# Layer 1's QKV projection: the bias through PE, the rotation of q and k on DVE alone

## The reference

```python
h = _layernorm(x) * (1 + ca) + sa
qkv = h @ w_qkv.T + b_qkv                      # 512 -> 768: 32 q heads, 8 k heads, 8 v heads of 16
q, k, v = split(qkv, [512, 640])
def apply_rope(x):                             # per head, pairs (even, odd)
    xr, xi = x[..., 0::2], x[..., 1::2]
    return stack([xr * cos - xi * sin, xr * sin + xi * cos])   # cos, sin of position * inv_freq, 8 values
q, k = apply_rope(q), apply_rope(k)
```

## Time and profile before

| | us |
|---|---|
| median of 3 runs (1818.61 to 1824.83) | 1823.09 |
| the profiled execution | 1821.3 |
| its span, first to last instruction | 1819.0 |
| PE busy | 1673.6 (92%) |
| DVE busy | 1203.1 (66%) |
| ACT busy | 1009.0 (55%) |
| POOL busy | 734.8 (40%) |

### The profile page before, as it was taken

The page is one execution under the profiler, slowest core; times in us unless marked ns, Lnnn a source line. Parts: engine busy times, 40 slices in busy tenths (PEclk is TensorE's granted clock), DMA queues, the critical chain, the costliest instruction groups (busy, mean ns, idle before and its releaser), DMA issues. The chain is left out here.

```text
span 1819.0 us, 28423 instructions
## 1 busy us (share of the span) xinstructions
PE 1673.6 (92%) x10091; PEld 1339.6 (74%) x10091; DVE 1203.1 (66%) x2930; ACT 1009.0 (55%) x2229; POOL 734.8 (40%) x660
## 2 busy tenths in 40 slices
PE   5599999999999999999997699997769999999778
PEld 3488999999999999899885588785645555554557
DVE  6867777777776777777667533345886777763475
ACT  3377777777777778777772311102216666666131
POOL 1486575766757567475531200000542222211200
PEclk9899999999999999999998799998959999999889
DMA  5000000100000100100002211005000000000021
GB/s 177 29 13 29 19 24 19 30 30 19 25 25 24 30 19 25 30 13 24 19 7 80 74 53 53 14 0 183 1 1 1 1 1 1 1 1 1 30 45 47
DMA packets 70772, 55.27 MB, mean 30 GB/s; under 512 B 22974, under 2 KB 52862, under 8 KB 70634
## 3 DMA queue, kind: packets, MB, share of 16 engines
q1 hardware_dynamic: 70634, 53.47, 10.0%
HBM read 51.36 MB, written 2.10 MB: 29 GB/s over the span
## 5 line engine op out<-in xcount | busy, mean ns | idle before, releaser
L698 PEld LDWEIGHTS psum<-a_probsT,a_v 128*128 128x128 f32 x2304 | 295.3, 192 | 25.5 <-issue 3.8
L698 PE MATMUL psum<-a_probsT,a_v 128*128 128x128 f32 x2304 | 299.9, 275 | 1.7 <-ACT a_probsT L896 1.5
L793 DVE CUSTOM_DVE_ANT_0 psum<-psum,a_keys_allowed 128x128 f32<-128x128 f32 (+7 forms) x256 | 195.7, 765 | 80.8 <-PE psum L77 72.0
L879 ACT ACTIVATE a_probs<-psum,a_neg_max 128x128 f32<-128x128 f32 (+7 forms) x256 | 190.8, 745 | 64.8 <-DVE a_neg_max L793 56.6
L1763 ACT ACTIVATE a_probsT<-psum 128x512 f32<-128x512 f32 (+3 forms) x384 | 174.2, 497 | 86.9 <-PE psum L1600 62.8
L888 ACT ACTIVATE a_probs<-a_probs,a_row_inv 128x128 f32<-128x128 f32 (+7 forms) x256 | 201.3, 786 | 21.9 <-DVE a_row_inv L800 21.4
L568 POOL TENSOR_TENSOR a_turned_pool<-a_q_sum,a_sine 64x512 f32<-64x512 f32 x62 | 79.3, 1279 | 273.3 <-DVE a_q_sum L779 272.1
L822 DVE TENSOR_TENSOR a_ctxT_lo<-psum,a_ctxT_hi 128x128 fp32r<-128x128 f32 x256 | 73.8, 288 | 173.8 <-ACT a_ctxT_hi L902 173.7
L896 ACT COPY a_probsT<-psum 128x512 f32<-128x512 f32 (+3 forms) x384 | 173.4, 488 | 18.4 <-PE psum L686 16.4
L812 DVE SCALAR_TENSOR_TENSOR a_sumT<-psum,a_scale_o,a_sumT 128x512 f32<-128x512 f32 x256 | 179.3, 743 | 0.9 <-PE psum L712 0.8
L686 PE MATMUL psum<-ident,a_probs 128*128 128x128 f32 x1152 | 168.9, 274 | 0.4 <-DVE a_q_sum L779 0.4
(11 more groups left out here) (306 smaller groups left out, 3935.3 us busy)
## 6 DMA issues: line engine op xcount, KB each, us to landing
a_raw_q<-in_L_attn_qw_q SPq DMA_DIRECT2D x32, 256.0 KB, 3.3
a_raw_o<-in_L_attn_qw_o SPq DMA_DIRECT2D x32, 256.0 KB, 2.8
mod1b_w<-in_L_wmod SPq DMA_DIRECT2D x4, 1024.0 KB, 11.2
mod0a_w<-in_L_wmod SPq DMA_DIRECT2D x3, 1024.0 KB, 10.6
mod0b_w<-in_L_wmod SPq DMA_DIRECT2D x3, 1024.0 KB, 7.8
f_raw<-in_L_ffn_down_w SPq DMA_DIRECT2D x10, 256.0 KB, 3.0
f_raw<-in_L_ffn_gate_w SPq DMA_DIRECT2D x10, 256.0 KB, 3.2
f_raw<-in_L_ffn_up_w SPq DMA_DIRECT2D x10, 256.0 KB, 3.5
```

Source lines behind the costliest of these rows:

```text
L698: last = nc.tensor.matmul(bank(use)[:, 0:P], v[:, g % 2, j, :], probsT[:, u % 2, j, :], start=(j == 0), stop=(j == i))
L793: nc.vector.tensor_tensor_reduce(out=scores, in0=scores, in1=keys_allowed[:, S - (i + 1) * P:S], scale=-1.0, scalar=-MASKED, op0=ALU.add, ...
L879: nc.scalar.activation(probs[:, u % 3, 0:(i + 1) * P], score[u % 2][:, 0:(i + 1) * P], ACT.Exp, bias=neg_max[:, h % 2, i:i + 1], scale=-1. ...
```

## The change

The bias is loaded as one row on one partition. POOL, before the loop, splits it into a high and a low part, makes a row of ones and a negated copy of the sine table, and is out of the loop. PE starts each accumulation with two matmuls of one row, ones by bias parts. DVE no longer adds the bias or copies the projection to SBUF: it reads q and k from PSUM, makes two products with the sine (320 columns each, the halves swapped), one with the cosine (640 columns) and one sum (640 columns). ACT copies v from PSUM. PE's wait for a free bank pair is on DVE's products and ACT's copy of v.

```diff
--- before.py
+++ after.py
@@ -1259,7 +1259,7 @@
         sem = lambda name: mem.semaphores.enter_context(nc.semaphore("p1_" + name))
         sb = lambda name, shape, dt=F32: ctx.enter_context(nc.sbuf_tensor("p1_" + name, shape, dt))
         raw = sb("raw", [P, NC, D])
-        bias = sb("bias", [P, QKV1])
+        bias = sb("bias", [1, QKV1])
         rope = sb("rope", [P, NT, 2, NP])
         w_in, small_in = sem("w_in"), sem("small_in")
 
@@ -1268,7 +1268,7 @@
                 modulation.load(sp, n)
             for c in range(NC):
                 sp.dma_start(raw[:, c, :], w_dram[c * P:(c + 1) * P, :]).then_inc(w_in, 16)
-            sp.dma_start(bias[:, :], b_dram.unsqueeze(0).broadcast_to([P, QKV1])).then_inc(small_in, 16)
+            sp.dma_start(bias[:, :], b_dram.unsqueeze(0)).then_inc(small_in, 16)
             sp.dma_start(rope[:, :, :, :], rope_dram.rearrange("(t p) a f -> p t a f", p=P)).then_inc(small_in, 16)
             for n in late.parts:
                 late.load(sp, n)
@@ -1277,37 +1277,16 @@
             modulation = Modulation(nc, mem, first, "mod1a", 1, (0, 1), wmod)
             layernorm_phase(nc, mem, 2, loads, modulation)
         wT = (sb("wT_hi", [P, KT, QKV1], F32R), sb("wT_lo", [P, KT, QKV1], F32R))
-        qkv = sb("qkv", [P, 2, QKV1])
-        part = [sb(f"part{n}", [P, NH, NP]) for n in range(4)]
-        roped = sb("roped", [P, 2, NH, HD1])
+        bias_part = [sb(f"bias_{of}", [1, QKV1], F32R) for of in ("hi", "lo")]
+        ones, ones_r, minus_sine = sb("ones", [1, P]), sb("ones_r", [1, P], F32R), sb("minus_sine", [P, NT, NP])
+        by_cosine, by_sine = sb("by_cosine", [P, NH, 2, NP]), sb("by_sine", [P, NH, 2, NP])
+        roped = sb("roped", [P, 2, NH, 2, NP])
         wT_turned, w_hi, w_split = sem("wT_turned"), sem("w_hi"), sem("w_split")
-        projected, biased, v_out = sem("projected"), sem("biased"), sem("v_out")
-        turned = {"even": sem("even_turned"), "odd": sem("odd_turned")}
-        summed = {"even": sem("even_summed"), "odd": sem("odd_summed")}
-        hi_done, split = sem("hi_done"), sem("split")
+        projected, turned, v_out = sem("projected"), sem("turned"), sem("v_out")
+        summed, hi_done, split = sem("summed"), sem("hi_done"), sem("split")
+        ready = sem("ready")
+        READY = 5
         block = ctx.enter_context(nc.Block())
-
-        def products(engine, which, t):
-
-            x = qkv[:, t % 2, 0:QK1].rearrange("p (h f two) -> p h f two", two=2, f=NP)
-            engine.wait_ge(biased, t + 1)
-            if t:
-                engine.wait_ge(summed[which], t)
-            for n in range(2):
-                cos_or_sin = rope[:, t, n if which == "even" else 1 - n, :].unsqueeze(1).broadcast_to([P, NH, NP])
-                last = engine.tensor_tensor(part[n if which == "even" else 2 + n][:, :, :], x[:, :, :, n], cos_or_sin, ALU.mult)
-            last.then_inc(turned[which], 1)
-
-        def combine(engine, which, t):
-
-            engine.wait_ge(turned[which], t + 1)
-            if t >= 2:
-                engine.wait_ge(hi_done, t - 1)
-                engine.wait_ge(split, t - 1)
-            a, b = part[0:2] if which == "even" else part[2:4]
-            columns = slice(0, NP) if which == "even" else slice(NP, HD1)
-            engine.tensor_tensor(roped[:, t % 2, :, columns], a[:, :, :], b[:, :, :],
-                                 ALU.subtract if which == "even" else ALU.add).then_inc(summed[which], 1)
 
         @block.tensor
         def _(pe):
@@ -1320,15 +1299,21 @@
                                                raw[:, c, k * P:(k + 1) * P], mem.ident[:, :])
                 last.then_inc(wT_turned, 1)
             for t in range(NT):
+                if t == 0:
+                    pe.wait_ge(ready, READY)
                 if t >= 2:
-                    pe.wait_ge(biased, t - 1)
+                    pe.wait_ge(turned, t - 1)
+                    pe.wait_ge(v_out, t - 1)
                 for cols in (slice(0, HALF), slice(HALF, QKV1)):
+                    for n in range(2):
+                        nc.tensor.matmul(mem.bank_pair4(t % 2)[:, cols], ones_r[:, :], bias_part[n][:, cols],
+                                         start=(n == 0), stop=False)
                     for k in range(KT):
                         if t == 0 and cols.start == 0:
                             pe.wait_ge(w_split, k + 1)
                         last = split_products(nc.tensor, mem.bank_pair4(t % 2)[:, cols],
                                               [a[:, k, t * P:(t + 1) * P] for a in mem.hT],
-                                              [a[:, k, cols] for a in wT], k == 0, k == KT - 1)
+                                              [a[:, k, cols] for a in wT], False, k == KT - 1)
                 last.then_inc(projected, 1)
 
         @block.scalar
@@ -1337,20 +1322,22 @@
                 act.wait_ge(wT_turned, k + 1)
                 nc.scalar.copy(wT[0][:, k, :], mem.bank_pair[k % 2][:, 0:QKV1]).then_inc(w_hi, 1)
             for t in range(NT):
-                act.wait_ge(biased, t + 1)
-                nc.scalar.copy(v1[:, t, :], qkv[:, t % 2, QK1:QKV1]).then_inc(v_out, 1)
-                act.wait_ge(summed["even"], t + 1)
-                act.wait_ge(summed["odd"], t + 1)
-                r = roped[:, t % 2, :, :].rearrange("p h d -> p (h d)")
+                act.wait_ge(turned, t + 1)
+                nc.scalar.copy(v1[:, t, :], mem.bank_pair4(t % 2)[:, QK1:QKV1]).then_inc(v_out, 1)
+                act.wait_ge(summed, t + 1)
+                r = roped[:, t % 2, :, :, :].rearrange("p h two f -> p (h two f)")
                 nc.scalar.activation(q1[0][:, t, :], r[:, 0:QW], ACT.Copy, scale=SCALE1)
                 nc.scalar.copy(k1[0][:, t, :], r[:, QW:QK1]).then_inc(hi_done, 1)
 
         @block.gpsimd
         def _(pool):
             pool.wait_ge(small_in, 32)
-            for t in range(NT):
-                products(pool, "odd", t)
-                combine(pool, "odd", t)
+            pool.memset(ones[:, :], 1.0).then_inc(ready, 1)
+            pool.tensor_copy(bias_part[0][:, :], bias[:, :]).then_inc(ready, 1)
+            pool.wait_ge(ready, 2)
+            pool.tensor_copy(ones_r[:, :], ones[:, :]).then_inc(ready, 1)
+            pool.tensor_tensor(bias_part[1][:, :], bias[:, :], bias_part[0][:, :].bitcast(F32), ALU.subtract).then_inc(ready, 1)
+            pool.tensor_scalar(minus_sine[:, :, :], rope[:, :, 1, :], -1.0, None, ALU.mult).then_inc(ready, 1)
 
         @block.vector
         def _(dve):
@@ -1358,27 +1345,34 @@
                 dve.wait_ge(w_hi, k + 1)
                 nc.vector.tensor_tensor(wT[1][:, k, :], mem.bank_pair[k % 2][:, 0:QKV1],
                                         wT[0][:, k, :].bitcast(F32), ALU.subtract).then_inc(w_split, 1)
-            dve.wait_ge(small_in, 32)
+            dve.wait_ge(ready, READY)
 
             def low(t):
                 dve.wait_ge(hi_done, t + 1)
-                dve.wait_ge(summed["odd"], t + 1)
-                r = roped[:, t % 2, :, :].rearrange("p h d -> p (h d)")
+                r = roped[:, t % 2, :, :, :].rearrange("p h two f -> p (h two f)")
                 nc.vector.scalar_tensor_tensor(out=q1[1][:, t, :], in0=r[:, 0:QW], scalar=SCALE1,
                                                in1=q1[0][:, t, :].bitcast(F32), op0=ALU.mult, op1=ALU.subtract)
                 nc.vector.tensor_tensor(k1[1][:, t, :], r[:, QW:QK1], k1[0][:, t, :].bitcast(F32),
                                         ALU.subtract).then_inc(split, 1)
 
             for t in range(NT):
+                x = mem.bank_pair4(t % 2)[:, 0:QK1].rearrange("p (h f two) -> p h f two", two=2, f=NP)
+                over_heads = lambda table: table.unsqueeze(1).broadcast_to([P, NH, NP])
                 dve.wait_ge(projected, t + 1)
+                if t:
+                    dve.wait_ge(summed, t)
+                for two in range(2):
+                    nc.vector.tensor_tensor(by_sine[:, :, two, :], x[:, :, :, 1 - two],
+                                            over_heads(rope[:, t, 1, :] if two else minus_sine[:, t, :]), ALU.mult)
+                nc.vector.tensor_tensor(by_cosine[:, :, :, :].rearrange("p h two f -> p h f two"), x,
+                                        rope[:, t, 0, :].unsqueeze(1).unsqueeze(3).broadcast_to([P, NH, NP, 2]), ALU.mult
+                                        ).then_inc(turned, 1)
+                dve.wait_ge(turned, t + 1)
                 if t >= 2:
-                    dve.wait_ge(v_out, t - 1)
-                    dve.wait_ge(turned["odd"], t - 1)
-                    dve.wait_ge(turned["even"], t - 1)
-                nc.vector.tensor_tensor(qkv[:, t % 2, :], mem.bank_pair4(t % 2)[:, 0:QKV1], bias[:, :], ALU.add
-                                        ).then_inc(biased, 1)
-                products(dve, "even", t)
-                combine(dve, "even", t)
+                    dve.wait_ge(split, t - 1)
```

(3 more changed lines are left out.)

## The result

The changed kernel is slower: median 1827.89 us of 9 runs (1826.23 to 1831.13) against 1820.91 of 9 runs before (1818.61 to 1824.83), a ratio of 1.0035 with a 95% interval of 1.0026 to 1.0044. That is 7 us, where 1.4 us less was forecast, and outside the range I gave (1817 to 1826). The forecast stood on the median of the first three runs of before, 1823.1; all nine give 1820.9, so 2.2 us of its number, 1821.7, is their scatter. The profiled execution took 1827.2 us, its span 1825.3.

The account below looks back on a forecast made before the run. DVE bounds the projection at 5.1 us a tile; PE would, at 4.91. PE through at 1315.7, DVE 0.27 later, plus 4.3: 1320.3 against 1321.7, 1.4 less, so 1821.7 us from median 1823.1; range 1817 to 1826.

Parts of the forecast that it names:

- PE became the bound: In the projection PE's tile of 4.91 us would exceed DVE's 3.27, so DVE waits some 1.6 us a tile.
- Undisturbed durations: DVE instructions in the projection without POOL beside them: 0.49 us for 320 columns, 0.69 for 512, 0.82 for 640.
- POOL was ready in time: POOL's preparation before the loop takes at most 4.9 us, to 1275.9, and PE asks at 1276.32.
- the first paragraph: In the projection DVE takes 5.1 us a tile, PE 4.2; relieving DVE returns no more than 0.9 us a tile.
- PE's part: Four added bias matmuls a tile in the projection cost PE 0.70 us, bounds 0 and 0.70, making its tile 4.91.
- The first rival: DVE's strided sine and cosine products cost twice per column: projection ends at 1321.6, 0.1 less than now, 1823.0 us; 12%.
- the 186 ns row: Profile row of a 16-element write with steps of 64 columns, 0.18 us plain; taken as evidence that strided writes cost the plain price.
- The slower rival: The same three DVE products cost above 2.3 times plain per column; at three times, +7.3 us, 1830.4 us; 4%.
- The free one-row matmul: PE's bias matmuls of one row cost nothing, its tile stays 4.21 us, 7.0 us less, 1816.1 us; 4%.
- The fourth: Clock behind the projection shifts as PE rests less: at most 3.9 us gained (1817.8, 7%) or as much lost (1825.2, 3%).

Follow-up runs that it names:

- the best variant: Kernel before, DVE still adding the bias, but rotation in four wide in-order instructions, POOL out of the loop, no bias matmuls: median 1814.02 us, ratio 0.9966.
- 128-row kernel: Changed kernel with bias matmuls contracting over all 128 rows, ones in row 0 and zeros below: median 1821.71 us against 1822.07, ratio 0.9999.
- the writes in order: 128-row kernel with rotated pairs kept side by side, so the cosine product reads and writes in order: one execution, 1825.1 us.
- The sweep: 128-row kernel with bias matmul rows differing by tile (1, 32, 33, 64, 65, 96, 97, 128): one execution, 1825.0 us.

## Why the prediction was wrong

**Right.** PE became the bound, DVE waits, and all it saves beyond PE's pace is covered. Undisturbed durations were read rightly: sine products 0.49, sum 0.82, low part 0.69 forecast; 0.49, 0.82, 0.68 measured. POOL was ready in time: 1274.1, bound 1275.9. No gain beyond 0.9 us a tile could be had from DVE, the first paragraph said, and the best variant got 0.87.

**The step that failed** is PE's part: "I see nothing that makes them dearer than matmuls of the same width". Its 0.70 us a tile was 1.50, and its bounds, 0 and 0.70, were open to below alone. The missing 0.80 is four changes between matmuls of up to 64 and of more than 64 rows, 0.2 us each. With 8 tiles that is 6.4 us, which turns the forecast 1.4 less into 5.0 more; the dear cosine product in the last tile adds 0.5: together 5.5, and the stage is 5.3 longer. The 128-row kernel is the test of the other steps: the part of its stage behind DVE's first start is 39.0 us, 38.6 with the writes in order, where they had given 1320.3 - 1281.6 = 38.7. The part ahead of it came out longer, 12.0 us against 1281.6 - 1271.0 = 10.6, as the clock rose late, a case that the prediction doesn't have; so its stage, 51.0 us, isn't shorter than the 50.7 of before. That its median, 1821.7, is the forecast to a tenth is luck: against 1822.1 of before in the same set it is 0.4 us less and not 1.4, a difference that these medians can't tell from none.

The page that would have told me is the Trainium skill's "TensorEngine Tiling (Array Packing)": Key Properties says that changing the tiling mode drains the engine, and Tiling Modes puts the modes at 128, 64 and 32 rows. The sweep agrees on where the line lies between 64 and 65; the price, 0.2 us a change, comes from these rows alone. That what is paid for is the page's drain is my reading; the runs show the place of the line and the price, and no row shows a drain as such. Between 32 and 33 rows, where by the page two modes part, both sides cost the same against 128-row neighbours (5.62 on the second tile, 5.71 on the third).

**The rivals.** The first rival, dear strided walks, came true by half: the sine products with every second column of PSUM cost nothing, the cosine product's alternating writes cost 1.8 times the time per column ((1331 - 160) / 640 = 1.8 ns against the plain 1.0). That half agrees with the page of the Trainium skill that I set against the change, "Advanced Engine Details and Errata", SBUF Cachelines; it was hidden by PE in all tiles but the last. And the 186 ns row, which I had set against the page, spoke for it. It lies 10 ns above my 0.16 + 16 x 0.001 = 0.176, and the kernel before has a product of the same 16 columns that writes in order:

```profile
L1706 DVE TENSOR_TENSOR a_neg_max<-a_neg_max 128x16 f32<-128x16 f32 x8 | 1.4, 175 | 0.3
```

11 ns over 16 writes are 0.7 ns each, and the cosine product paid (1331 - 814) / 640 = 0.8. I had judged a price for each write by its total on a row too short to show it. The slower rival came out in its sign and not by its mechanism. I had looked for a slowdown only in DVE's prices, though PE was to be the bound; there every 0.1 us a tile counts in full. The free one-row matmul, 4%, was the very opposite of the fact. The fourth, the clock behind the stage, came out faintly on its good side: over the first 60 us behind the stage the mean granted clock was 0.68 before, 0.76 and 0.72 in the two executions after, and the attention's first write of `attended` came 56.4 us behind the stage's end before, 55.6 and 56.1 after. That is 0.3 to 0.7 us of the 3.9 that I had allowed. The two executions of the 128-row kernel lie on the bad side, at 57.9 us. Of the 7.0 us between the medians 5.3 are shown in the stage; the rest isn't located. It is of the size of the scatter in the clock's rise, which alone makes 3 us between the two executions of the changed kernel, and of that behind the stage.

## What to carry to other kernels

Where a change moves the bound from one engine to another, the prices on the new bound's engine are the ones to take apart, and an added instruction of a kind that the trace doesn't hold needs an upper bound above its plain price. A matmul over 64 rows or fewer in a stream of 128-row ones costs two changes, 0.4 us here whether it is one row or 64: pad it with zeros to more than 64 rows, which cost nothing beyond its columns here (4.91 us a tile, as reckoned from the columns). Taking POOL off work that reads SBUF beside DVE, with wider instructions on DVE, was worth 0.9 us a tile (0.67 of that the low part of q alone) with no work given to PE; that part of the change by itself is the faster kernel.

## What the runs showed of the hardware that I had not expected

- Going from matmuls over more than 64 rows to matmuls over 64 or fewer, or back: 0.1 us before the first matmul of the new kind and 0.1 behind it. Four a tile took PE from 4.91 to 5.71 us, two to 5.32. Among 65, 96, 97 and 128 rows nothing that counts: 4.90 to 4.94.
- A DVE product of 640 columns that writes alternately 32 bytes apart: 1331 ns; in order 814. With every second column as input in PSUM or as output in SBUF, 320 columns take 480 to 492 ns, the plain price.
- The clock's rise at the start of this stage came 4, 8 or 11 us after PE's first transpose in executions of like kernels, and at two of these points for one and the same: 11.4 and 14.3 us to DVE's first start in two executions of the changed kernel, 11.3 and 9.9 with the bias on DVE.
- The same code behind the stage took 494.4 to 501.2 us in fourteen executions; between the ends PE was busy 440.5 and 449.2 us for the same 2676 matmuls, at a mean granted clock of 0.93 and 0.91, in the shortest and the longest.
